# One wait for each score product and for each maximum in a windowed attention

## The reference, cut to what matters

```
scores = q @ k^T                 # keys of this tile and of its neighbours, outside the window masked
p      = exp(SC * (scores - max over the row))
o      = (p @ v) / sum(p)
x      = x + gate * (o @ Wo)
```

## Time and profile before

| | us |
|---|---|
| median of 3 runs | 3168.64 (3160.45 to 3170.83) |
| the profiled execution | 3166.53 |
| its span, first to last instruction | 3164.8 |
| TensorE matmuls busy | 3051.6 (96%) |
| VectorE, ScalarE busy | 1947.1 (62%), 1725.4 (55%) |
| the changed stage | about 1141 to 1700 of the span |

### The profile page before, as it was taken

The page is one execution under the profiler, slowest core; times in us unless marked ns, Lnnn a source line. Parts: engine busy times, 40 slices in busy tenths (PEclk is TensorE's granted clock), DMA queues, the critical chain, the costliest instruction groups (busy, mean ns, idle before and its releaser), DMA issues. The chain is left out here.

```text
span 3164.8 us, 49386 instructions
## 1 busy us (share of the span) xinstructions
PE 3051.6 (96%) x16544; PEld 1895.5 (60%) x16545; DVE 1947.1 (62%) x4607; ACT 1725.4 (55%) x3807; POOL 764.8 (24%) x1037
## 2 busy tenths in 40 slices
PE   8999998999999989999998999999999999998999
PEld 4455555569999953333334666665555666665555
DVE  6999995652333346666664777885333777777342
ACT  6776762223333326665665888885222777776221
POOL 1111113650000035554533232221011111112111
PEclk9999999999999989999999999999999999999999
DMA  9900004131111121111101000000001000000000
GB/s 329 321 1 1 1 1 159 47 104 52 46 48 48 40 77 25 30 30 29 26 14 42 11 11 9 11 7 32 1 0 36 9 11 10 10 8 5 14 14 27
DMA packets 114254, 134.12 MB, mean 42 GB/s; under 512 B 14478, under 2 KB 100342, under 8 KB 113786
## 3 DMA queue, kind: packets, MB, share of 16 engines
q1 hardware_dynamic: 106042, 109.57, 10.7%
q0 software_dynamic: 7872, 21.77, 2.2%
q10 hardware_dynamic: 128, 0.10, 0.0%
HBM read 60.33 MB, written 60.83 MB: 38 GB/s over the span
## 5 line engine op out<-in xcount | busy, mean ns | idle before, releaser
L1946 DVE CUSTOM_DVE_ANT_0 sb_win_masked<-ps_win_pss,sb_win_around 128x384 f32<-128x384 f32 (+1 forms) x512 | 256.3, 538 | 174.3 <-PE ps_win_pss L2074 172.3
L2386 ACT ACTIVATE sb_loc_pr<-ps_loc_psw,sb_loc_nb,sb_loc_sc 128x256 f32<-128x256 f32 x512 | 281.0, 569 | 135.9 <-DVE sb_loc_nb L2531 135.9
L2613 PE MATMUL ps_stk_banks<-sb_stk_w,sb_loc_hT 128*128 128x512 f32 x768 | 346.6, 601 | 2.7 <-ACT sb_loc_hT L2353 2.7
L1808 ACT ACTIVATE sb_win_pT<-ps_win_pst 128x512 f32<-128x512 f32 x368 | 199.8, 596 | 172.1 <-PE ps_win_pst L2085 117.3
L1530 PE MATMUL ps_exp_ps<-sb_exp_xT,sb_exp_here 128*128 128x128 f32 x2272 | 266.3, 276 | 0.5 <-ACT sb_exp_xT L1439 0.5
L2074 PE MATMUL ps_win_pss<-sb_win_kT,sb_win_q 32*128 32x384 f32 (+1 forms) x1024 | 233.9, 528 | 31.2 <-DVE sb_win_qtok L1946 20.5
L1530 PEld LDWEIGHTS ps_exp_ps<-sb_exp_xT,sb_exp_here 128*128 128x128 f32 x2272 | 260.3, 193 | 0.8 <-ACT sb_exp_xT L1439 0.7
L2613 PEld LDWEIGHTS ps_stk_banks<-sb_stk_w,sb_loc_hT 128*128 128x128 f32 x768 | 140.6, 190 | 176.8 <-issue 176.8
L755 PE MATMUL ps_rec_psp<-sb_rec_hT,sb_rec_w 128*128 128x512 f32 x512 | 232.6, 598 | 0.8 <-DVE sb_keep_modf L546 0.8
L2908 DVE SCALAR_TENSOR_TENSOR sb_mlp_hid<-ps_stk_banks,sb_stk_col,sb_mlp_gl 128x512 f32<-128x512 f32 (+1 forms) x112 | 75.1, 672 | 245.7 <-ACT sb_mlp_gl L2863 245.5
L2085 PE MATMUL ps_win_pst<-sb_win_qm,sb_win_kT 32*128 32x512 f32 x736 | 216.6, 662 | 1.5 <-ACT sb_win_pT L1808 1.5
(11 more groups left out here) (372 smaller groups left out, 6702.8 us busy)
## 6 DMA issues: line engine op xcount, KB each, us to landing
sorted_tokens<-sb_rec_blank SPq DMA_DIRECT2D x9, 4224.0 KB, 30.4
sb_exp_rows<-sorted_tokens SPq DMA_DIRECT2D x71, 128.0 KB, 2.0
expert_results<-sb_exp_res SPq DMA_DIRECT2D x71, 128.0 KB, 1.7
sb_moe_w_in<-in_L_ffn_w_in_eDF SPq DMA_DIRECT2D x8, 512.0 KB, 10.7
sb_moe_w_sw<-in_L_ffn_w_swiglu_eDF SPq DMA_DIRECT2D x8, 512.0 KB, 10.8
sb_exp_w_out<-in_L_ffn_w_out_eFD POOLq DMA_DIRECT2D x8, 512.0 KB, 9.0
sb_stk_angles<-in_angles SPq DMA_DIRECT2D x32, 128.0 KB
sb_stk_xs_b<-sb_stk_y SPq DMA_DIRECT2D x64, 63.5 KB
```

The lines of the kernel that those rows point to most:

```text
L1808: nc.scalar.activation(pT[:, n % PARTS], pst[:, n % TURNED], ACT.Exp, scale=SC).then_inc(s_e, 1)
L1946: nc.vector.tensor_tensor_reduce(masked[:, pair % 2, j, 0:keys], pss[:, (n + j) % PLAIN, 0:keys], around[:, first:first + keys], 1.0, -3e3 ...
L2386: e = nc.scalar.activation(pr[:, hf, h], psw[:, hf, h // 2, h % 2 * 256:h % 2 * 256 + 256], ACT.Exp, scale=sc8[:, b, hh:hh + 1], bias=nb[: ...
L2613: t = nc.tensor.matmul(psa[:, c], hT[:, b, k, 1 - k:P + 1 - k], w[:, k, c * 512:(c + 1) * 512], start=(k == 0), stop=(k == KD - 1))
```

## The change

TensorE's two helpers that waited for both maxima and both exponentials ahead of a slot are gone. Each product now has one wait of its own directly ahead of it. On VectorE, each maximum waits for its own plain product.

```diff
@@ maxima (VectorE)
                     n = u * AH + 2 * k
                     g, c = in_order(2 * k)
-                    dve.wait_ge(s_s, n + 2)
                     first, pair = 0 if where(u)[1] else P, n // 2
                     if pair >= 2:
                         dve.wait_ge(s_top, 2 * (pair - 1))
                     for j in range(2):
+                        dve.wait_ge(s_s, n + j + 1)
                         nc.vector.tensor_tensor_reduce(masked[:, pair % 2, j, 0:keys], pss[:, (n + j) % PLAIN, 0:keys],
@@ TensorE
-                def maxima_done(u, k):
-                    for j in range(2):
-                        n = u * AH + 2 * k + j
-                        if n >= PLAIN:
-                            pe.wait_ge(s_top, n - PLAIN + 1)
-
-                def exps_done(u, k):
-                    for j in range(2):
-                        n = groups_before(u) * 4 + 2 * k + j
-                        if n >= TURNED:
-                            pe.wait_ge(s_e, n - TURNED + 1)
-
                 def scores(u, k, j):
...
                     n = u * AH + 2 * k + j
+                    if n >= PLAIN:
+                        pe.wait_ge(s_top, n - PLAIN + 1)
                     g, c = in_order(2 * k + j)
...
                     n = groups_before(u) * 4 + 2 * k + j
+                    if n >= TURNED:
+                        pe.wait_ge(s_e, n - TURNED + 1)
                     c = ((2 * k + j) % 4 + 2) % 4
...
-                        if 0 <= s < NT:
-                            maxima_done(s, k)
-                        if turned:
-                            exps_done(s - 1, k - 2)
                         for j in range(2):
                             if 0 <= s < NT:
                                 scores(s, k, j)
```

## The result

The changed kernel takes 3149.72 us (median of 6 runs, 3144.59 to 3150.76); the kernel before 3168.52 (6 runs, 3160.45 to 3170.83). The ratio is 0.9946, with an interval of 0.9933 to 0.996. Two more pairs gave 0.994 [0.9918, 0.9962] and 0.9953 [0.9935, 0.9971]. So it is 0.5 to 0.6% faster, some 14 to 19 us. The forecast of 3164 was wrong: it counted on 2.8 us. That low end stood there for the rival "the clock stays up". So it says nothing for the forecast's sum that its range ends where the result lies; that is luck. What happened is that rival, whose gain is partly taken back later, with as much again from closed gaps and from waits that the forecast had put at nothing.

A forecast was written before the change was run, and what follows sets the result against it. TensorE, busy 96% of the span, was taken as the bound. Gains of 1.57 us (steps 1, 2, 17, 18) and 1.2 us (last three steps) summed to 2.8 us, giving 3164 us, with a range of 3151 to 3173.

The forecast's parts named there:

- the clock stays up: Rival: low clock spells after slot 2's gap in steps 1, 2, 17, 18 vanish; 11.2 us, giving 3152.5; chance 0.20.
- The ceiling: TensorE's idle time ahead of plain score products, 30.5 us or about 1%, caps any gain at unchanged clock.
- The title's half of the routing: First half of the change's title, experts and routing: nothing in the diff touches them, counted as zero.
- Steps 1, 2, 17 and 18 without the clock: Steps without a values product in slot 1: earlier S0 and T0 close gaps around slots 2, 3 and 6; 1.57 us.
- Slots 3 and 6 of an even step: Gaps of 0.40 and 0.18 us stay, since T1 still waits for its exponential; gain 0, at most 0.02 per gap.
- the change shortens nothing of the second: In slot 3 the second release, the exponential's, already waited for T0 alone; T1 still starts 0.75 us after it.
- Slot 1: Even step, no turned products: S0 goes 0.20 us earlier, but VectorE's division passes nothing on; gain 0.
- The last three steps: Slots 2 to 4 lack full-array products between them, so sets overlap and exponentials start earlier: 0.4 us each, 1.2 us.
- Waits cost nothing: TensorE executes as many waits as before, a met one costing 0 to 0.01 us; VectorE has slack; counted 0.
- waits pull the set apart: Slower rival: met waits between side-by-side products delay the second, 3179 us at 25 ns; chance of waits costing something 0.12.
- The even gaps close too: Rival: all 0.78 us of gaps go in 27 even steps, 21 us, giving 3142.6; chance 0.07.
- Nothing moves: Rival: the last steps' gain is lost behind DMAs moving sums and outputs; 3166.5 us; chance 0.11.

The follow-up runs named there:

- turned alone: Kernel before, but each turned product has its own wait for its exponential, both maxima still awaited ahead of the set: 3169.42 us, ratio 1.0019.
- VectorE alone: Kernel before with only VectorE's part of the change, each maximum waiting for its own plain product: 3164.17 us, ratio 1.0001.
- the moved wait: Kernel before with VectorE's part; TensorE keeps one later wait per pair ahead of the set, the exponential's carried by S0: 3160.85 us, ratio 0.999.
- the kernel with spins: Kernel before, waits untouched, plus five unused identity transposes ending slot 1 in steps 1, 2, 17 and 18: 3158.7 us, ratio 0.9982.
- the same spins in both kernels: Unused identity transposes at the stage's end: in the kernel before (also spins in steps 1, 2, 17, 18) 3154.44 us; in the changed kernel 3143.7 us.
- the tripled ones: Changed kernel with every product's wait stated three times: 3157.53 us, ratio 0.9978 to the kernel before; the changed kernel of its group took 3147.83.

## What of the prediction held and what failed, point by point

*The ceiling and the reading of the stage* held. TensorE is the bound, and what moved outside the stage (1.8 and -2.0 us) is for the most part low clock in unchanged code. The title's half of the routing counted as zero, and nothing in the trace speaks against it.

*The clock.* The forecast put its gain at nothing. It said that a spell comes at all four places, so it isn't a close decision, and gave the rival 0.20. That step failed. In the four profiled executions that keep the gap (before, turned alone, VectorE alone, the moved wait), 10 of 16 places had a spell (4, 3, 2 and 1); in the ten in which S0 and T0 start early or spins fill slot 1, 2 of 40. Both of these, and three of the ten, are the fall of step 1, which begins ahead of the gap of slot 2 or of what fills it. In steps 2, 17 and 18 it is 7 of 12 against 0 of 30: that is what shows that the filled gap keeps the clock. The argument against the rival compared the width of what moves. That was no evidence: five transposes of 0.76 us in all sufficed. The steps with a spell differed from the even ones, which kept their clock with gaps of 0.2 to 0.4, by the missing values product and the gap of 0.7 in its place; I should have weighed that above the regularity of the fall, which one execution showed and three others did not. Which of the two it is, the missing work or the idle time, spins can't tell, for they change both; the changed kernel, which adds no work and has no spell at the three places, speaks for the idle time.

The rival's price was right in sum, 11.2 us worked out and 11.25 measured, and partly by luck: for step 1 it is 4.0 and 4.05, but step 2 cost 2.79 where 4.0 stood for it, and 17 and 18 together 4.41 where it was 3.2. It is the price where all four spells come.

The rule of the Trainium skill that the prediction cited ("TensorE: Matmul & The Clock Gate", section "Why this matters for your kernels") would have made this gain zero. The same page, in the section "A second HAM failure mode: psum-queue depth-cycling", tells of a kernel whose short idle times between groups of products made the clock swing, without a length. This trace agrees with that section and not with the rule: in steps 2, 17 and 18 of the kernel before the clock fell in or behind gaps of 0.71 us (the one of step 18 is in the earlier trace rows).

*Steps 1, 2, 17 and 18 without the clock:* 1.57 us forecast. Measured against the kernel with spins, which has the full clock and all other gaps: 31.69 - 29.99 = 1.70 and 32.20 - 31.03 = 1.17, together 2.87. The mechanism was right. The sizes were taken with a part of the gaps at low clock, and the 0.1 of each slot 6 was not in them.

*Slots 3 and 6 of an even step:* gain 0, at most 0.02, forecast; 0.20 for the whole step measured, and over 25 even steps 5 us. (The prediction counts 27 from step 3 to 29, but 17 and 18 are not even.) The failed step is "the change shortens nothing of the second". The 0.75 from exponential to T1 was taken as the exponential's own time. 0.10 of it was the separate wait in between, and its being the same 0.75 in the last step was no proof, since the same helper waited there. It is 0.65 in the changed kernel. That the maximum and the exponential end together in slot 3 was right, and irrelevant for a half of it: the projection behind that set is held by `modulate`, behind the exponentials on ScalarE, so the gap that the record shows ahead of slot 3 could not be gained from its own end, and what moved the projection was T0 of slot 2. I had looked for who releases the set, and not for who releases what follows it.

*Slot 1* gained next to nothing for the slot behind, as forecast: the values product starts 2.52 us into the step, and 2.54 before. The maximum of slot 0 has 0.72 us behind it there (1245.43 to 1246.15), not the 0.70 of slot 3.

*The last three steps:* 0.4 us for each was forecast. Step 30, at full clock in both kernels, gained 0.7, in sets that overlap as described; with the same spins in both kernels, steps 30 and 31 together gained 1.2 and the rest of the stage 0.4. So the term was too small rather than too large, but the low clock takes 3.7 back from step 31 to the start of the next stage. That it could fall where it had not fallen before was not among my cases.

*Waits cost nothing.* This held for the changed kernel, and for the wrong reason: TensorE does not execute as many as before. The row with 1248.05 and 1248.06 shows a wait that T0 itself carries, and that TensorE had reached during the values product. The change takes 405 separate waits away, and where one is left or added behind a release it costs about 0.1 us, as the turned waits alone and the tripled ones show. The rival "waits pull the set apart" is what those two kernels do.

*The even gaps close too:* 0.07, and a quarter of it came true (0.20 of 0.78). *Nothing moves:* no.

Measured and forecast, summed: forecast 2.8 us. For this pair of executions: the clock, 11.25 at four places; gaps at these places 2.87; even steps 4.9; step 30 0.7; less 3.7 from step 31 on. That is 16.0, and with the +1.8 and -2.0 of unchanged code the 15.8 of the spans. Net of what the stage's end takes back, the clock is 7.5 of it and the closed gaps and waits 8.5, somewhat less than the 9 to 11 us at equal mean clock. The steps that failed are two, then: the clock's gain put at nothing, and the exponential's 0.75 taken as its own time.

Open: why the clock falls at the stage's end more in the changed kernel than before, where the same gaps of 0.77 us stood in the last steps. Its mean clock is 0.91 in 1643 to 1700, and 0.79 after, in a stretch that there holds the end of this stage and the start of the next. That spins there save it is shown; why the kernel before escaped a part of it without them is not, nor what makes the clock of step 1 fall in some executions and not in others.

## What to carry to other kernels

Where the granted clock falls again and again at one place of a regular schedule, compare that place with its neighbours that keep it: what differs is the candidate, and a few products without use put there show what the clock is worth. Take several profiled executions, and look in each whether the fall comes ahead of the place or behind it: one execution with four spells had made the fall look certain here. And compare runs at the same mean clock, to see what the change is worth without it. When a gap ends at a release, read on to the next full-array product and ask what releases *it*; only that gap can be gained. Put the wait that ends last on the product itself, as its only one, and have waits that are surely met stand behind a long product, where they cost nothing here.

## What the runs showed of the hardware that I had not expected

- TensorE's granted clock went to its lower level (1.2 GHz) in or behind gaps of about 0.7 us in 7 of 12 cases (steps 2, 17 and 18), and in none of 30 where spins of 0.76 us or early products filled the gap. It also fell with no gap in the record just ahead: in step 1 in 5 of 14 executions, while TensorE was busy with slot 1 or 2, and at 1645 in the changed kernel, busy for the 5 us before.
- From the start of an exponential to the product that it releases: 0.75 us with a separate wait instruction, 0.65 with the wait on the product. From a maximum: 0.72 in slot 1 of the kernel before (1245.43 to 1246.15), where no exponential is waited for, and 0.61 and 0.62 in the changed one (1236.44 and 1238.05, in the rows below, to S1 at 1237.05 and 1238.67).
- Some gaps are not in the record. The values product of slot 1 is listed with 1.07 us in both kernels, and slot 2 follows it after 1.06 us before and after 0.99 in the changed one: 0.07 us of waiting lay under a modelled end. The maximum that the set waited for, in a row of VectorE at 1247.40, started 0.65 us ahead of it.

```profile
1236.44 0.55 DVE L1946 CUSTOM_DVE_ANT_0 sb_win_masked<-ps_win_pss,sb_win_around 128x384 f32<-128x384 f32 x1
...
1238.05 0.56 DVE L1946 CUSTOM_DVE_ANT_0 sb_win_masked<-ps_win_pss,sb_win_around 128x384 f32<-128x384 f32 x1
```
